# One shared semaphore for the accumulating output writes, and no wait that its engine has made before

## The reference

```
L_q = exterior(xn @ W1_q.T, xn @ W2_q.T)      # 16 heads, 6 numbers a head, normalised
L_k = exterior(xn @ W1_k.T, xn @ W2_k.T)
scores = einsum('bqhc,bkhc->bhqk', L_q, L_k @ J6.T) * 6**-0.5   # causal
attn = softmax(scores);  v = xn @ W_v.T + b_v
out = einsum('bhqk,bkhd->bqhd', attn, v).reshape(B, T, D) @ W_out.T + b_out
ffn: W_real, W_imag = two 512x512 matrices unfolded from G1, G2
     out_real = xr @ W_real.T - xi @ W_imag.T;  out_imag = xr @ W_imag.T + xi @ W_real.T
```

## Time and profile before

| | |
|---|---|
| times of 3 runs | 4605.42, 4621.39, 4632.08 us (median 4621.39) |
| the profiled execution's own time | 4613.27 us |
| span of its slowest core (core 5) | 4612.2 us |
| spans of the 8 cores | 4570.2 to 4612.2 us |
| mean granted PE clock of the cores | 0.654 to 0.660 of full |
| busy on core 5 | PE 61%, ACT 32%, DVE 30%, POOL 3% |

### The profile page before, as it was taken

One profiled execution on the slowest core, in us unless ns is written; L12 is line 12 of the kernel. 1 busy time (PEld: TensorE's weight loads), 2 busy tenths in 40 slices (PEclk: granted clock), 3 DMA queues, 4 the chain that ended last, 5 costly groups with the idle time before them and its releaser, 6 DMA issues.

```text
span 4612.2 us, 36015 instructions; the slowest of 8 cores (4570.2 to 4612.2 us)
## 1 busy us (share of the span) xinstructions
PE 2819.9 (61%) x10528; PEld 976.0 (21%) x10528; DVE 1384.2 (30%) x2833; ACT 1475.4 (32%) x1729; POOL 140.4 (3%) x210
## 2 busy tenths in 40 slices
PE   2358555566655955556655685556665587666667
PEld 1115111121211521112211341112221152111112
DVE  4524433332222333332322343333222232111112
ACT  0000144433332024443333104444433203555451
POOL 2200000000000000000000010000000000000001
PEclk9959655567656865656765785556776586555557
DMA  5701311012200231012110050011220013000004
GB/s 113 48 0 55 98 32 30 28 46 66 68 9 10 32 63 28 28 35 64 64 42 7 8 79 29 28 35 37 70 68 14 5 19 62 14 12 12 14 12 78
DMA packets 87144, 180.26 MB, mean 39 GB/s; under 512 B 41760, under 2 KB 42920, under 8 KB 86960
## 3 DMA queue, kind: packets, MB, share of 16 engines
q0 software_dynamic: 56672, 75.38, 8.9%
q1 hardware_dynamic: 30288, 102.58, 7.6%
HBM read 114.36 MB, written 69.73 MB: 40 GB/s over the span
## 4 chain that ended last, share of the span: by engine, by line
PE 45%; DMA 19%; DVE 15%; ACT 12%; issue 8%; DVEq 1%; SPq 0%; ACTq 0%; POOLq 0%; POOL 0%
PE O L575 18%; DMA cdiv<-rscr 10%; PE S L535 7%; PE F L405 5%; ACT exps L558 5%; DMA y<-ost 4%; DMA rscr<-cdiv 3%; DVE oT L617 3%; PE F L441 3%; ACT cdiv L601 3%; ACT cdiv L599 3%; PE F L448 2%; PE F L331 2%; DVE exps L566 1%; PE F L311 1%
## 5 line engine op out<-in xcount | busy, mean ns | idle before, releaser
L558 ACT ACTIVATE exps<-S 128x1024 bf16<-128x1024 f32 (+3 forms) x1280 | 1120.7, 894 | 2003.7 <-PE O L575 1352.0
L575 PE MATMUL O<-exps,vaug 128*65 128x512 bf16 (+3 forms) x2560 | 1041.7, 508 | 841.2 <-DVE oT L617 499.6
L535 PE MATMUL S<-fqp,fkp 6*128 6x512 bf16 (+3 forms) x2560 | 620.7, 494 | 428.3 <-ACT exps L558 421.7
L575 PEld LDWEIGHTS O<-exps,vaug 128*65 128x65 bf16 x2560 | 230.9, 136 | 1284.8 <-issue 1266.1
L617 DVE TENSOR_TENSOR oT<-O,cdiv 64x512 bf16<-64x512 f32 x256 | 174.9, 683 | 920.4 <-DMA cdiv<-rscr 914.5
L535 PEld LDWEIGHTS S<-fqp,fkp 6*128 6x128 bf16 x2560 | 141.3, 97 | 1147.6 <-issue 1141.6
L566 DVE TENSOR_TENSOR exps<-exps,tri 128x256 bf16<-128x256 bf16 x512 | 142.9, 290 | 738.0 <-ACT exps L558 735.5
L405 PE MATMUL F<-wv,xnT 128*128 128x256 bf16 x2048 | 249.4, 281 | 0.9 <-DVE vaug L417 0.6
L481 PE MATMUL S<-wout,oT 128*128 128x512 bf16 x1024 | 228.6, 382 | 16.9 <-DVE oT L617 9.1
L311 PE MATMUL F<-idt,xnst 128*128 128x128 f32 x512 | 121.2, 416 | 149.3 <-DVE xnst L298 149.3
L405 PEld LDWEIGHTS F<-wv,xnT 128*128 128x128 bf16 x2048 | 191.2, 100 | 64.1 <-issue 28.8
(11 more groups left out here) (75 smaller groups left out, 1939.5 us busy)
## 6 DMA issues: line engine op xcount, KB each, us to landing
y<-ost POOLq DMA_DIRECT2D x128, 512.0 KB, 5.2
x2st<-x SPq DMA_DIRECT2D x64, 512.0 KB, 4.3
cdiv<-rscr SPq DMA_DIRECT2D x128, 256.0 KB, 3.7
xst<-x SPq DMA_DIRECT2D x56, 512.0 KB, 4.5
exps<-x SPq DMA_DIRECT2D x8, 512.0 KB, 4.3
wv<-wvT POOLq DMA_DIRECT2D x8, 256.0 KB, 23.0
wout<-woutT POOLq DMA_DIRECT2D x8, 256.0 KB, 23.7
tascr<-qk POOLq DMA_DIRECT2D x16, 128.0 KB, 2.0
```

The source lines that it names most:

```text
L535: tS.inc(TE.matmul(S_ps[:, ss * 1024 + j * 512 + soff: ss * 1024 + j * 512 + 512], fk_pad[32 * m4:32 * m4 + 6, kt * 128:kt * 128 + 128], f ...
L558: sS.inc(SE.activation(e_out, e_in, AF.Exp))
L575: ins = TE.matmul(O4[:, j * 512 + off:(j + 1) * 512], vaug[:, kt * 1040 + h * 65: kt * 1040 + h * 65 + 65], exp_sb[:, ss * 1024 + j * 512 ...
```

## The change

Two things are changed, and one function is added.

1. `Sem.wait` remembers for each engine the highest value that the engine has already waited for on this semaphore, and puts no instruction when the new value isn't higher.
2. The semaphore `dyb` is gone. All accumulating writes signal `dya`, and POOL waits, before it issues one, for the last one issued, whatever its p.
3. `OutProjPart` is defined and called nowhere.

```diff
 class Sem:
...
     def wait(self, eng, n=None):
-        eng.wait_ge(self.h, self.n if n is None else n)
+        v = self.n if n is None else n
+        k = id(eng)
+        if self.lastw.get(k, -1) >= v:
+            return
+        self.lastw[k] = v
+        eng.wait_ge(self.h, v)
...
-        dtr, dyb = sems["dtr"], sems["dyb"]
-        DYA = [dya, dyb]
+        dtr = sems["dtr"]
...
-            dyb.wait(VE, stx["ost_ra"][1])
+            dya.wait(VE, stx["ost_ra"][1])
...
         def burst_outproj(b):
...
-                DYA[p].wait(VE, stx["ost_ra"][p])
+                dya.wait(VE, stx["ost_ra"][p])
...
                 vS.wait(GE, cp_s)
-                DYA[p].wait(GE, stx["dya_last_p"][p])
-                stx["dya_last_p"][p] = DYA[p].inc(GE.dma_start(y_d[b, tt * 128:(tt + 1) * 128, :],
-                                                               ostage[:, p * 1024:(p + 1) * 1024],
-                                                               accum_op=OP.add), 16)
-                stx["ost_ra"][p] = stx["dya_last_p"][p]
+                dya.wait(GE, stx["dya_last"])
+                stx["dya_last"] = dya.inc(GE.dma_start(y_d[b, tt * 128:(tt + 1) * 128, :],
+                                                       ostage[:, p * 1024:(p + 1) * 1024],
+                                                       accum_op=OP.add), 16)
+                stx["ost_ra"][p] = stx["dya_last"]
...
-        dyb.wait(SY)
```

More of the change, by code:

```diff
@@ L80, in __init__ @@
         self.n = 0
+        self.lastw = {}
     def inc(self, instr, k=1):
@@ L170, in build @@
         sems = {}
-        for name in ["dwp", "dxp", "dws", "dyt", "dx", "dx2", "dyp", "dya", "dbo", "dbi", "dtr", "dyb", "t", "v", "s"]:
+        for name in ["dwp", "dxp", "dws", "dyt", "dx", "dx2", "dyp", "dya", "dbo", "dbi", "dtr", "t", "v", "s"]:
             sems[name] = Sem(st, nc, "sem_" + name)
@@ L200, in build @@
             "ost_ra": [0, 0],
-            "dyp_last": 0, "dya_last_p": [0, 0],
+            "dyp_last": 0, "dya_last": 0,
             "unfold_t": 0,
@@ L471, in FFN_pass1, with OutProjPart @@
             stx["ost_rp"][1] = stx["dyp_last"]
+        def OutProjPart(b, g, tt):
+            p = tt % 2
+            vS.wait(TE, max(stx["f_r"][0], stx["f_r"][1], stx["odiv"]))
+            sS.wait(TE, max(stx["f_rs"][0], stx["f_rs"][1]))
+            for half in range(2):
+                Fb = FB[half]
+                for k2 in range(2):
+                    pt = 2 * g + k2
+                    ins = TE.matmul(Fb[:, 0:512],
+                                    oT[:, pt * 2048 + tt * 128: pt * 2048 + tt * 128 + 128],
+                                    wout_sb[:, pt * 1024 + half * 512: pt * 1024 + half * 512 + 512],
+                                    start=(k2 == 0), stop=(k2 == 1))
+                tS.inc(ins)
+                stx["f_w"][half] = tS.n
+            for half in range(2):
+                tS.wait(VE, stx["f_w"][half])
+                if half == 0:
+                    dyp.wait(VE, stx["ost_rp"][p])
+                    dya.wait(VE, stx["ost_ra"][p])
+                stx["f_r"][half] = vS.inc(VE.tensor_copy(
+                    ostage[:, p * 1024 + half * 512: p * 1024 + half * 512 + 512], FB[half][:, 0:512]))
+            cp_s = vS.n
+            vS.wait(GE, cp_s)
+            dya.wait(GE, stx["dya_last"])
[3 more added lines that the diff above has]
+            stx["ost_ra"][p] = stx["dya_last"]
         def burst_outproj(b):
```

## The result

| | before | after |
|---|---|---|
| median | 4613.39 us (8 runs) | 4682.21 us (8 runs) |
| lowest, highest | 4600.55, 4632.08 | 4675.81, 4692.06 |
| profiled span of the slowest core (core 5 in both) | 4612.2 | 4680.7 |
| bursts 1 to 3, first write to last copy | 54.8, 56.3, 54.6 | 86.3, 84.9, 84.4 |
| burst 4, first write to the end of the span | 61.0 | 96.5 |

The ratio of after to before is 1.0147, with a 95% interval of 1.0127 to 1.0168: slower by 68 us, forecast 68. The forecast median was 4689, because it started from the median of three runs, 4621; eight runs of before have 4613. (A ninth run of after, 4706.24 us, is on record outside the eight.) In the profiles the bursts together are 125.4 us longer (352.1 against 226.7) and the rest is 56.9 us shorter; 125.4 - 56.9 = 68.5, the difference of the two spans.

A forecast was written before the change was run, and what follows sets the result against it. It took many handoffs between engines, with no engine full, to bound the kernel. Bursts +116 us and waits taken out -48 us gave +68 us, a median of 4689 us; forecast 4665 to 4715 (0.60), range 4645 to 4730.

The forecast's parts named there:

- The round of the burst: Output projection bursts: one landing, 5.3, plus POOL's reaction, 0.54, so 5.84 us a tile in place of 3.65; together +116 us.
- The burst before: Bursts 1 to 3, first write to last copy: taken as 51.3, 56.3 and 54.6 us before the change.
- A write that is alone lands no sooner: Burst writes: a lone landing taken as 5.3 us, the steady burst's figure; with 4.64 the bursts would cost 80 us.
- rival 1: Burst writes: alone, a write lands much sooner, 4.0 us or less; chance 0.05 for no change, 0.04 for a gain.
- The waits taken out, 48 us: Met waits removed across the kernel, priced where they stand on the path: -48 us, lower end 30, upper end 80.
- Division: The 128 divisions, all in the chain: waits removed on DVE, SP and, 48 times, ACT save 17.8 us.
- V: The 256 tiles of V: two waits go from a weight-load gap with room for four; half of 24 taken, 12.2 us.
- Preparation of sequence 0: Before V of sequence 0: 7.4 us saved, 5.4 for the tiles and a quarter of 8.0 for B1 and B2.
- B2: 32 steps on PE: two second waits go, 0.20 us a step together, saving 6.4 us.
- 4 (6.1): Burst writes that are alone land later, 6.1 us as at a burst's start: +111, 4732 us; chance 0.08.
- 2 (80 us of waits and more): Removed waits worth far more, 80 giving 4657; 0.12 for 4640 to 4665, short landings included, 0.03 for no change.
- 3, PE's clock: PE's clock falls to its lower level in the bursts, at most 64 us more: 4753 us; chance 0.08.

The follow-up runs named there:

- the four partial runs: Kernel before, two semaphores, met waits left out in V_group, the division, the preparation or the rest alone: 0.9993, 0.9929, 0.9946, 0.9988.

## Why the prediction was right, and where its parts were off

The forecast and the measured difference are both 68 us. That is partly luck: the burst cost 9 us more than forecast (125.4 against 116), and the waits taken out gave back 9 more (56.9 against 48). The mechanisms were right and both sums too small. Point by point:

- *The round of the burst is one landing and POOL's reaction.* Shown, by the chain after, and by the run with one semaphore alone (+123). Reaction 0.53 (0.54 forecast). Landing: this is the term that was too small. The four bursts of after sum to 352.1 us and 339.4 were forecast (3 x 82.1 + 93.1); 12.7 / 54 = 0.24 us more in each step, so that a landing took 5.5 and not 5.3 us. The median of the landings is 5.5.
- *The burst before.* I misread one number. The earlier trace rows give 1637.78 as the last copy of burst 1, but that is the 15th of 16. The last starts at 1641.30, so the burst was 54.8 us and not 51.3, and the sum should have been 116 - 3.5 = 112.5. Measured 125.4. The missing 13 us are the longer landings. The misreading hid 3.5 of them. Single bursts also spread: with two semaphores and no low clock the sum of four was 220.6 to 231.5 us in the other profiles, before 226.7. This row follows later in the timeline of before:

```profile
1641.30 1.22 DVE L490 COPY ost<-S 128x1024 f32<-128x1024 f32 x1 [2.30 <-DMA y<-ost]
```

- *A write that is alone lands no sooner.* Shown for the accumulating write, by the median of 5.5. The lower bound of 4.64 came from the wrong kind of write, and as evidence against rival 1 it was worth nothing. The trace of before had the answer: its plain writes (L469) landed in 2.9 us at the least, its accumulating ones in 5.1. It did no harm, since the row of the lone write, 5.5, was right.

```profile
DMA to landing us min/median/max: 2.9/3.8/8.9
```

- *The waits taken out, 48 us.* 57 measured (44 to 69). Division 19 us by its stretch (17.8 forecast). V 15 at equal clock (12.2 forecast, half the gap; in the running stream it is that half, 0.05 us a tile). Preparation of sequence 0: 8.6 (7.4 forecast). B2 as priced, by its rows. That leaves some 14 of the 57, for which the forecast had 10.5 (B1 and B2 of the other three sequences, the feed-forward tiles); they are within the noise of the four partial runs, and not settled.
- *Rivals.* 1 (landings of 4.0 or less) and 4 (6.1) are out by the median of 5.5. 2 (80 us of waits and more) is out: the interval of the run that leaves them out ends at 69. 3, PE's clock: its mechanism was there and cost next to nothing. The bursts of after had a granted clock of 0.86 to 0.91, before 0.95 to 1.00, and some tiles took 5 us on PE, but the copies still waited for DMA, except the first two of a burst and one more: a round of 6.1 us has room for such a tile. With two semaphores it hasn't. In two bursts of the run that leaves out V's waits alone, and in two of the run that leaves out those of the preparation, the clock was 0.81, all copies waited for PE, a tile took 4.2 us, and the burst 61.2 where others took 52 to 57. My argument against this rival was also weak: the row with a clock of 1.00 is one of six stretches of the same feed-forward tiles, and four of the others had 0.74 to 0.84. What kept the price low was the slack of the round, not a clock that stays high. Burst 1 of after, and such a stretch of before (columns as in the earlier trace rows):

```profile
1552.00:1633.00 81.00, 59.71 (x234) 23.81 (x232) 16.23 (x14) 0.00 (x0) 11.09 (x13) 0.89 0.56 85
...
490.00:510.00 20.00, 13.31 (x41) 4.79 (x42) 7.21 (x19) 0.00 (x0) 1.59 (x3) 0.74 0.38 121
```

The DMA engines were busy 56 to 58% of the bursts of after. Before it was 85 to 92%; the 83% of the earlier trace rows is of a window that reaches 9 us beyond the burst. It is work of much the same size over a longer time.

## What to carry to other kernels

A wait that is already met is not free: find the handoffs on the path and count the wait instructions behind the one that ends late, or in front of an engine that is never idle. Two semaphores for two buffers are what lets two transfers fly at once; merging them turns the time of a tile from half a round into a whole landing. Price such an edit with the same kind of transfer, accumulating or plain, alone or beside others, and add up the two edits by themselves before judging their sum.

## What the runs showed of the hardware that I had not expected

- An accumulating write of 512 KB to memory lands in 5.5 us, a plain one in 2.9, both alone on their core.
- With four places to stage, the landing is longer (median 5.9 us) but a tile leaves every 3.46 us, so that about two writes are in flight at a time (5.9 / 3.46). The DMA engines are shown as busy all the time. That was no bound at this rate, as all copies waited for PE; what a faster PE would find, no run shows. By the same column a plain write kept them busy some 1.2 us (0.36 x 3.46, an estimate), an accumulating one 3.5 (1.01 x 3.46):

```profile
1543.00:1594.00 51.00, 50.07 (x232) 22.50 (x230) 18.12 (x15) 0.00 (x0) 12.78 (x15) 1.00 1.01 146
```

- A met wait cost 0.07 us on DVE and 0.05 on SP behind a late one; on PE 0.10 behind a late one and 0.05 in a running stream, taken out or put in. Four more of them on DVE cost 0.38 us in a division instead of 0.28.
